# Mamba scan stage of a sandwich block: convolution by stacked taps in four column groups, two copies moved to VectorE, a third dBx buffer

## What is computed

```
xc   = silu(causal_conv(x, w[4 taps]) + b)
dt   = softplus(dt_w @ proj(xc)[:64] + dt_b)        B, C = rest of proj(xc), 16 states each
h[n] = exp(dt * A[n]) * h[n] + (dt * xc) * B[n]     (a scan over time, n = 0..15)
y    = sum over n of h[n] * C[n] + D * xc
```

## Time and profile before

| | us |
|---|---|
| median of 3 runs (4640.19 to 4651.91) | 4651.12 |
| the profiled execution | 4640.61 |
| its span, first to last instruction | 4638.7 |
| input projection and front of the scan stage | 0 to 250.8 |
| the 16 units of the scan | 250.8 to 2059 |

### The profile page before, as it was taken

How to read it: one execution, slowest core, us unless ns; L and a number is a source line. 1 busy time by engine, 2 the same in 40 slices (tenths; PEclk the granted TensorE clock), 3 DMA queues, 4 the chain that set the end, 5 groups by cost and what they waited for, 6 DMA issues and landing times. The chain is left out here.

```text
span 4638.7 us, 68636 instructions
## 1 busy us (share of the span) xinstructions
PE 3669.2 (79%) x20726; PEld 2241.8 (48%) x20726; DVE 2843.6 (61%) x4186; ACT 2755.0 (59%) x4377; POOL 1717.7 (37%) x1132
## 2 busy tenths in 40 slices
PE   8488888888888888866776888888988885499990
PEld 4256666666666666654553222222222223366660
DVE  4268787777777787756675666666666665411105
ACT  3289898988989898964663455555555551011110
POOL 0067777777777777763342000000000002300006
PEclk9799999999989999987886899999999997699995
DMA  6311111111111111114645000000000103311115
GB/s 209 111 44 58 56 56 56 65 56 56 56 56 56 56 60 61 56 74 152 214 154 163 17 24 24 26 24 20 24 26 24 26 17 116 122 61 68 69 41 184
DMA packets 151474, 329.26 MB, mean 71 GB/s; under 512 B 17443, under 2 KB 92310, under 8 KB 136656
## 3 DMA queue, kind: packets, MB, share of 16 engines
q1 hardware_dynamic: 97392, 229.08, 14.6%
q10 hardware_dynamic: 39760, 51.81, 3.3%
q0 software_dynamic: 13968, 43.97, 2.8%
HBM read 216.45 MB, written 110.91 MB: 71 GB/s over the span
## 5 line engine op out<-in xcount | busy, mean ns | idle before, releaser
L671 DVE TENSOR_TENSOR_SCAN scan_hh<-scan_dA,scan_state,scan_bx 128x512 f32<-128x512 f32 x1024 | 1247.1, 1265 | 390.5 <-PE scan_bx L755 350.2
L471 POOL TENSOR_TENSOR scan_hC<-scan_hh,scan_cbc 128x1024 f32<-128x1024 f32 x512 | 1208.2, 2369 | 309.2 <-DVE scan_hh L671 234.2
L1403 DVE TENSOR_REDUCE attend_mx<-attend_s 128x1 f32<-128x512 f32 (+1 forms) x1360 | 781.3, 608 | 343.3 <-PE attend_s L1533 225.1
L755 PE MATMUL scan_bx<-kept_ident,scan_dBxT 128*128 128x128 f32 x4096 | 671.7, 290 | 151.4 <-DVE scan_hh L671 125.3
L755 PEld LDWEIGHTS scan_bx<-kept_ident,scan_dBxT 128*128 128x128 f32 x4096 | 518.0, 150 | 416.0 <-issue 207.9
L538 ACT ACTIVATE scan_dBxT<-scan_dtxT,scan_bt 128x512 f32<-128x512 f32 x1028 | 655.9, 712 | 83.4 <-PE scan_bx L755 83.2
L533 ACT ACTIVATE scan_dA<-scan_dt,scan_an 128x512 f32<-128x512 f32 x1028 | 655.4, 711 | 0.0
L765 PE MATMUL scan_acc<-kept_ident,scan_hC 128*128 128x128 f32 x4128 | 648.2, 284 | 1.3 <-POOL scan_hC L471 1.3
L1497 ACT ACTIVATE attend_full<-attend_s 128x1024 f32<-128x1024 f32 x384 | 392.0, 1025 | 333.4 <-PE attend_s L1560 329.4
L1533 PE MATMUL attend_s<-attend_kt,attend_qt 96*128 96x512 bf16 (+1 forms) x1360 | 483.6, 373 | 130.4 <-DVE attend_mx L1403 72.6
L765 PEld LDWEIGHTS scan_acc<-kept_ident,scan_hC 128*128 128x128 f32 x4128 | 517.3, 149 | 1.6 <-POOL scan_hC L471 1.6
(11 more groups left out here) (218 smaller groups left out, 4597.6 us busy)
## 6 DMA issues: line engine op xcount, KB each, us to landing
scan_cbc<-scratch_crows SPq DMA_DIRECT2D x64, 1024.0 KB, 4.7
scratch_qk<-mix_heads ACTq DMA_DIRECT2D x64, 384.0 KB, 10.0
scan_xw<-scratch_xin SPq DMA_DIRECT2D x18, 1030.0 KB, 7.3
scratch_y<-scan_uu ACTq DMA_DIRECT2D x17, 1024.0 KB, 3.9
attend_qt<-scratch_qk SPq DMA_DIRECT2D x34, 384.0 KB, 3.7
attend_kt<-scratch_qk SPq DMA_DIRECT2D x34, 384.0 KB, 4.4
mix_yf<-scratch_y SPq DMA_DIRECT2D x10, 1024.0 KB, 8.2
mix_yb<-scratch_y SPq DMA_DIRECT2D x10, 1024.0 KB, 11.8
```

The lines of the kernel that those rows point to most:

```text
L471: pool.tensor_tensor(hC[n % 2][:, ms, :], h[:, ms, :], rows.unsqueeze(1).broadcast_to([P, 2, C]), ALU.mult).then_inc(hc_ok, 1)
L671: dve.tensor_tensor_scan(hh[n % 2][:, m, r], dA[n % 2][:, m, r], bx[bank(j)][:, r], state[:, d, n, m:m + 1], ALU.mult, ALU.add).then_inc(h ...
L755: last = pe.transpose(bx[bank(j)][:, t * P:(t + 1) * P], dBxT[n % 2][:, t, m * P:(m + 1) * P], k["ident"][:, :])
L1403: dve.tensor_reduce(mx[:, t, c:c + 1], s1[v % 2][:, 0:w], AX_X, ALU.max).then_inc(s1_read, 1)
```

## The change

1. **Convolution.** The input of a tile is now loaded four times, once for each tap and shifted by it, into 32 partitions each (`xs[tap*32 ...]`), so that the 128 partitions hold 4 taps of 32 channels, and the free dimension has the 4 groups of channels. One product with a 128x32 stationary operand then sums all four taps of 32 channels. Four such products write 32 partitions of `fr` each.
2. **Loads.** A unit's input comes in 4 tiles of 4 DMAs (256 KB each) in place of one DMA of 1030 KB. `xs` has two buffers, one for even and one for odd tiles. SP's order changes: store and load C first, then tiles 0 and 1, then C groups 2 and 3, then tiles 2 and 3, each behind the convolution that frees its buffer.
3. **VectorE** takes the Relu of each dt product (ScalarE keeps the Abs, which now waits for `relu_ok`) and the four copies of turned dt*x.
4. **Third dBxT buffer.** `spread_b` waits for an earlier n.
5. **Front re-ordered.** All four convolutions of a unit now run in the unit two before it. `silu` moves from after n = 3 to after n = 0, the projection from sub-steps 19 to 22 to 7 to 10, the dt products from 29, 31, 33, 35 to 18, 21, 24, 27, GpSimd's add from after n = 9 to after n = 6, and VectorE's three long passes, before after n = 10, 10, 11, now stand after n = 8, 9, 10. On ScalarE exp, 1+e, log and several copies now stand between `spread_b` and `decay` (`middle`).
6. **Chunks** are unrolled in Python on all engines; only the loop over the two batches is left.

```diff
-        xw = [s.sb(f"xw{i}", [P, DT, C + HALO]) for i in range(2)]
-        diag = s.sb("diag", [P, 2, DT, TAPS, P])
+        xs = [s.sb(f"xs{i}", [P, COLS, C]) for i in range(2)]
+        pick = s.sb("pick", [P, STRIP])
+        taps = s.sb("taps", [P, 2, DT, COLS, STRIP])
...
-        dBxT = [s.sb(f"dBxT{i}", [P, JT, DI]) for i in range(2)]
+        dBxT = [s.sb(f"dBxT{i}", [P, JT, DI]) for i in range(3)]
...
-        FR_CONV, FR_PROJ, FR_BT, FR_DT, FR_NEXT, FR_TURN, FR_ALL = 0, 2, 3, 4, 8, 10, 14
+        FR_PROJ, FR_BT, FR_DT, FR_NEXT, FR_TURN, FR_LAST, FR_ALL = 0, 1, 2, 6, 9, 13, 14
+        FR_BEGIN = 18
+        AT_DT, AT_NEXT, AT_TURN, AT_LAST, AT_SKIP = (18, 21, 24, 27), (30, 36, 41), (49, 51, 53, 55), 58, (14, 16, 19, 22)
...
-                with eng.Fori(0, NC) as c:
+                for c in range(NC):
...
+                for tap in range(TAPS):
+                    o = at + tap
+                    sp.dma_start(xs[m % 2][tap * STRIP:(tap + 1) * STRIP, :, :], xinv[b, m, :, :, o:o + C]
+                                 ).then_inc(loaded_x[m % 2], 16)
...
+            for m in range(2):
+                load_x(0, 0, 0, m)
+            for m in range(2, DT):
+                sp.wait_ge(fr_mm, m - 1)
+                load_x(0, 0, 0, m)
+            for m in range(2):
+                sp.wait_ge(fr_mm, m + 3)
+                load_x(0, 0, 1, m)
+            for m in range(2, DT):
+                sp.wait_ge(fr_mm, 14 + m - 1)
+                load_x(0, 0, 1, m)
...
+                        store_c(f, d)
+                        sp.wait_ge(stored_c, f * 16 + 16)
+                        for g in range(2):
+                            load_c(f, d, g)
+                        sp.wait_ge(fr_mm, first)
                         hold(sp, k)
+                        for m in range(2):
+                            load_x(nb, nc_, d, m)
+                        for g in range(2, 4):
+                            load_c(f, d, g)
+                        for m in range(2, DT):
+                            sp.wait_ge(fr_mm, first + FR_NEXT + m - 1)
+                            hold(sp, k)
+                            load_x(nb, nc_, d, m)
...
-                act.wait_ge(fr_mm, group + 1)
-                act.activation(ee[:, m, :], fr[:, :], ACT.Abs, bias=db[:, d, m:m + 1])
-                act.activation(dt[d][:, m, :], fr[:, :], ACT.Relu, bias=db[:, d, m:m + 1]).then_inc(fr_out, 1)
+                act.wait_ge(relu_ok, f * DT + m + 1)
+                act.activation(ee[:, m, :], fr[:, :], ACT.Abs, bias=db[:, d, m:m + 1]).then_inc(fr_out, 1)
...
+                def middle(n):
+                    if n == 2:
+                        for half in range(2):
+                            evacuate(f, half)
+                    if n == 3:
+                        proj_out(g, first + FR_PROJ)
+                    if n == 4:
+                        bt_out(o, first + FR_BT)
+                    if n in (5, 6):
+                        dt_out(o, g, n - 4, first + FR_DT + n - 4)
+                    if n == 7:
+                        front_exp(g, first + FR_DT + 3)
+                    if n == 8:
+                        front_one_plus(g)
+                    if n == 9:
+                        front_log(g)
+                    if n == 11:
+                        conv_out(d, f + 2, 2, first + FR_NEXT + 2)
+                    if n == 15:
+                        conv_out(d, f + 2, 3, first + FR_LAST)
+
+                def tail(n):
+                    if n == 0:
+                        silu(o, g, first - 1)
+                    if n == 3:
+                        store(f)
+                    if n == 4:
+                        dt_out(o, g, 0, first + FR_DT)
+                    if n == 6:
+                        dt_out(o, g, 3, first + FR_DT + 3)
+                    if n in (8, 9):
+                        conv_out(d, f + 2, n - 8, first + FR_NEXT + n - 8)
+
...
-                    act.wait_ge(bx_mm, q * DT + HELD_BX)
+                    act.wait_ge(bx_mm, f * SUB + turned_free(n + 1 if n + 1 < NS else NS))
                     spread_b(dn, at)
+                    middle(n)
                     for m in range(DT):
                         decay(dn, q + 1, at, m)
+                    tail(n)
...
+            def relu(d, f, m, group):
+                if m == 0 and not (isinstance(f, int) and f == 0):
+                    dve.wait_ge(dt_ok, f)
+                dve.wait_ge(fr_mm, group + 1)
+                dve.tensor_scalar(dt[d][:, m, :], fr[:, :], db[:, d, m:m + 1], 0.0, ALU.add, ALU.max
+                                  ).then_inc(relu_ok, 1)
+
+            def turned_out(d, j, group):
+                dve.wait_ge(fr_mm, group + 1)
+                dve.tensor_copy(dtxT[d][:, j, :], fr[:, :]).then_inc(fr_out, 1)
+
...
-            def conv(d, group, nth, m, taps):
-                for j in taps:
-                    if j == 0:
-                        if m == 0:
-                            pe.wait_ge(loaded_x[d], nth * 16 + 16)
-
-                        if not (isinstance(group, int) and group == 0):
-                            pe.wait_ge(fr_out, group)
-                    o = j if d == 0 else HALO - j
-                    last = pe.matmul(fr[:, :], diag[:, d, m, j, :], xw[d][:, m, o:o + C], start=j == 0,
-                                     stop=j == TAPS - 1)
-                    if j == TAPS - 1:
-                        last.then_inc(fr_mm, 1)
+            def conv(d, group, u, m):
+                pe.wait_ge(loaded_x[m % 2], (u * 2 + m // 2 + 1) * 16 * TAPS)
+
+                if not (isinstance(group, int) and group == 0):
+                    pe.wait_ge(fr_out, group)
+                for g in range(COLS):
+                    last = pe.matmul(fr[g * STRIP:(g + 1) * STRIP, :], taps[:, d, m, g, :], xs[m % 2][:, g, :],
+                                     start=True, stop=True, skip_group_check=True)
+                last.then_inc(fr_mm, 1)
```

More of the change, by code:

```diff
@@ L420, in _ @@
                         f = (b * NC + c) * 2 + d
-                        sp.wait_ge(fr_mm, f * FR_ALL + 4)
-                        hold(sp, k)
[L424 to L437, removed]
+                        first = f * FR_ALL + FR_BEGIN
+                        nb, nc_ = (b, c + 1) if c + 1 < NC else (1 - b, 0)
+                        store_c(f, d)
[3 more added lines that the diff above has]
+                        sp.wait_ge(fr_mm, first)
+                        hold(sp, k)
+                        for m in range(2):
[6 more added lines that the diff above has]
+                            load_x(nb, nc_, d, m)
         @block.gpsimd
@@ L454, in _ @@
                 pool.memset(state[:, :, :, :], 0.0).then_inc(zeroed, 1)
-                with pool.Fori(0, NC) as c:
+                for c in range(NC):
                     for d in range(2):
@@ L564, in _ @@
             front_log(0)
-            for j in range(JT):
-                turned_out(0, 0, j, 10 + j)
-            for m in range(2):
+            for m in range(DT):
                 conv_out(1, 1, m, 14 + m)
@@ L581, in unit @@
                     if n + 1 == NS:
-                        act.wait_ge(fr_out, first + FR_ALL)
-                    act.wait_ge(bx_mm, q * DT + HELD_BX)
+                        act.wait_ge(fr_out, first + FR_TURN + JT)
+                    act.wait_ge(bx_mm, f * SUB + turned_free(n + 1 if n + 1 < NS else NS))
                     spread_b(dn, at)
-                    if n == 2:
-                        for half in range(2):
-                            evacuate(f, half)
+                    middle(n)
                     if n + 1 == NS:
@@ L655, in times_x @@
                 dve.tensor_tensor(dtx[:, :, :], dt[d][:, :, :], xc[d][:, :, :], ALU.mult).then_inc(front_ok, 1)
+            def relu(d, f, m, group):
[7 more added lines that the diff above has]
+                dve.tensor_copy(dtxT[d][:, j, :], fr[:, :]).then_inc(fr_out, 1)
+            for m in range(DT):
+                relu(0, 0, m, 6 + m)
             softplus_low(0, 0)
@@ L659, in _ @@
             times_x(0, 0)
+            for j in range(JT):
+                turned_out(0, j, 10 + j)
             def scan(d, f, n, m):
@@ L679, in unit @@
                         scan(d, f, n, m)
+                        at = n * DT + m
+                        if at in AT_DT:
+                            i = AT_DT.index(at)
+                            relu(o, g, i, first + FR_DT + i)
+                        if at in AT_TURN:
+                            i = AT_TURN.index(at)
+                            turned_out(o, i, first + FR_TURN + i)
+                    if n == 8:
+                        softplus_low(o, g)
+                    if n == 9:
+                        softplus(o, g)
                     if n == 10:
[L681 to L683 removed]
                         times_x(o, g)
@@ L738, in _ @@
             for m in range(DT):
-                conv(0, m, 0, m, range(TAPS))
+                conv(0, m, 0, m)
```

(6 more changed lines are left out.)

115 lines of the change are left out of this document (51 added, 64 removed).

## The result

The changed kernel took 4655.88 us (median of 20 runs, 4643.95 to 4669.53) against 4642.63 for the kernel before in the same session (20 runs, 4627.99 to 4652.63). The ratio is 1.003, interval 1.0019 to 1.004. The forecast was 4512, range 4430 to 4600. The profiled execution has a span of 4654.6 us.

A forecast was written before the change was run, and what follows sets the result against it. ScalarE was taken as the bound: 96.2 us work plus 8.3 idle gives a 104.5 us unit; 16 units plus 3.4 make 1675 against 1808, -133. With +4 for the front, 4640.6 becomes 4512, range 4430 to 4600.

The forecast's parts named there:

- the jumps back: Chunk loop: engines start late at each jump back; seven such boundaries, one remains, for which 3.4 us is added.
- the front: Before the first scan: cheaper diagonals against later loads of tiles 2 and 3, net -7 to +15 us, taken as +4.
- TensorE's 9.6 us a unit: Four convolutions a unit: column groups run beside each other, 9.6 us less TensorE work, priced at nothing since TensorE isn't the bound.
- The third dBxT buffer takes away the wait for TensorE: Before `spread_b`: third buffer removes ScalarE's wait, but `decay` waits for the scan instead; alone it earns 0 to 2.92 us.
- the 5.2 us a unit: ScalarE's wait for TensorE before `spread_b` in the kernel before, 83.2 us over 16 units, forecast to go.
- the 0 to 2.92: Range in us for what the third dBxT buffer earns alone, as `decay`'s wait for the scan two states back remains.
- The lateness of tile 2: Load of x for sub-step 41: ready 19.2 to 22.2 us after exp, needed at 20.2; late by 0 to 2, taken 1.0.
- first sign of being wrong: TensorE idle before its third convolution of a unit, with a DMA as releaser, for over 3 us.
- The rival of the late pieces: x loads: four pieces in a row take 14.8 us, not 7.3, so the tile is 9.5 late; 4648 us, chance 9%.
- the surplus of VectorE's busy half: n = 8 to 14: VectorE's extras 14.0 less ScalarE's 5.7 and the 4.7 lead leave ScalarE waiting 3.6 us a unit.
- before Abs (3.2 forecast): dt products: Abs waits for Relu, Relu for the third next scan; ScalarE waits 3.2 us a unit, bounds 0 and 8.8.
- the rival of the single bank: `fr` bank: ScalarE a block behind VectorE makes each of four Abs 2.45 us late, 9.8 a unit; 4669 us, chance 7%.

The follow-up runs named there:

- e8: e4 with only the four Relus of a unit back on ScalarE, VectorE keeping the copies: 4455.2 us, ratio 0.9604.
- e1: Changed kernel with the unit-end spread of B waiting for n = 12 to be turned instead of n = 15: 4586.77 us, ratio 0.988.
- e15: e8 with the wait at the unit's end as strict as in the changed kernel: 4527.07 us, ratio 0.975.
- e7: e4 with dBxT in two buffers as before: 4501.32 us, ratio 0.9692.
- e14: e8 with dBxT in two buffers as in the kernel before: 4462.51 us, ratio 0.9609.
- e2: Changed kernel with ScalarE's copies of the first two convolutions behind the decays of n = 7 and 8, not 8 and 9: 4631.27 us, ratio 0.998.
- e3: Changed kernel with tiles 2 and 3 of x loaded before C's fourth group: 4608.13 us, ratio 0.9938.
- e4: Changed kernel with e1, e2 and e3 together: 4499.43 us, ratio 0.97.
- the three edits: e1, e2 and e3 together on the changed kernel, run as e4: 4499.43 us, ratio 0.97.
- e12: Changed kernel as it is, with only the four Relus of a unit back on ScalarE: 4622.21 us, ratio 0.9953.
- e13: e8 with ScalarE emptying the accumulator earlier, behind n = 1: 4453.26 us, ratio 0.9595.

## Why the prediction was wrong

**What held.** ScalarE is the engine nearest to the unit's length, and the change takes 4 us of its work away: 96.7 measured, 96.2 forecast. The convolution's eight records take 1.06, the jumps back cost 28 us for 20, the front 2.8 for 4. TensorE's 9.6 us a unit are saved too, as e8's 83.2 against 92.8 shows; in the changed kernel, with more of it at the lower clock, it is busy for 86.4.

**The step that failed.** "The third dBxT buffer takes away the wait for TensorE", and with it the 5.2 us a unit, was wrong: the wait rose to 8.7. The buffer was read from what the edit is for, and its slots at the unit's end were not worked out. Two spreads wait there. The one for n = 15 writes the slot of n = 13, two states back as with two buffers: 4.1 of the 8.7 us. The one for the next unit's first state takes its count from `turned_free(16)`, the slot of n = 15, and so waits for all 64 sub-steps, while with two buffers it stopped at n = 14: 4.6 us. This second one is 69 us of the kernel's time (e1), and 72 with the rest mended (e15). With that count mended, the buffer as it stands in this ring is worth nothing (e7 and e14), the lower end of the 0 to 2.92 that the prediction gave it by itself.

**The step that was left out.** The prediction followed the `fr` bank through the dt products, but not through the convolutions: the first one's product stands at sub-step 30, the second's at 36, and between them ScalarE's copy stands behind the decays of its step n = 8. TensorE arrived 6.5 us too early, every unit (e2, 25 us alone).

**A term that was mis-sized.** The lateness of tile 2 was 4.8 us in the unit shown and 3.9 on average, not 1.0 (e3, 48 us alone); this was the prediction's own first sign of being wrong. The supply was right: from the end of exp at 869.8 to TensorE's start at 891.6 are 21.8 us, forecast 19.2 to 22.2. The demand was wrong: TensorE wanted the tile at 886.8, 17.0 after exp, not 20.2. VectorE's long passes took 2.29 and 2.98 in that unit, not 4.4. The price that the prediction took from the Trainium skill, "SBUF — State Buffer", section "Door 1: The DMA port swizzle", and left out of its sum, was 13.6 us for the four pieces of a tile, 6.3 more than for one load. The trace doesn't bear it out: TensorE starts on tile 2 at 891.57, 9.2 us after the first of its pieces was issued at 882.34. One load of 1030 KB landed in 7.3 before; a single piece of 256 KB takes a median of 7.8 (6.3 in e3), so a piece is no faster than the whole, but the pieces overlap. The rival of the late pieces (4648) came nearest to the measured time by chance: the lateness it rests on, 9.5 us, did not come.

**Two agreements that are luck.** The first is the 3.4 us of `decay` behind the scan, forecast at 3.6 as the surplus of VectorE's busy half. It shrinks to 2.0 us a unit in e2 and 1.1 in e3 and is gone in e4, with VectorE's work all in place: it came from TensorE's two stands, not from VectorE's passes. The second is the sum. The changed kernel's 4656 less the three edits is 4499, where 4512 was forecast, and e4 has 7.9 us of idle time a unit for 8.3. But 4.7 of it are before Abs (3.2 forecast) and 3.0 before the spread for n = 15 (nothing forecast), while the 3.6 for VectorE's busy half and the 1.0 for tile 2 are gone. Two terms too small and two too large nearly cancel.

**The moved work.** (It is four Relus and four copies a unit; the "two copies" of the title are the two kinds.) Two costs were put on the eight operations: their work, hidden under ScalarE's, and 3.2 us before Abs. The wait was 4.5. But taking the Relus back gave 34 us here (e12) and 44 with the three edits (e8), though ScalarE then works 2.0 us a unit more. Priced against the sum of work, a Relu on VectorE saves 0.57; in the measured time, that saving included, it costs 44 / 64 = 0.7 for each of the 64 Relus. It goes with the wait before Abs, which falls from 4.7 us a unit to 0.3. Abs stands behind Relu by the program's choice; whether both could read the bank unordered for less was not tried.

**Together.** The convolution's hold and the Relu hand-over are of the kind of the rival of the single bank (4669), but the largest cause, e1, is none of it; no rival had it. What e2 and e3 are worth with only the other missing was not tried. Nor was the clock taken apart from the waits: the mean granted clock of the scan stage was 0.93 before, 0.90 in the changed kernel, 0.94 in e4 and 0.95 in e8, so part of what the edits give back may be TensorE's faster work once it stands less.

The version that beats both kernels is e8 (4455.2, ratio 0.9604), or e13, which is the same within its spread.

## What to carry to other kernels

Where several engines run hand-ordered programs through one bank or one ring of buffers, work out for each waiting instruction its count at the wrap-around, and for each group in which position of which program the releaser stands. A sum of work said that some 130 us were to be had, and e4 has some 140; one wrong index, one copy a state too late and one load behind another took all of it back. Look twice before two readers of one PSUM bank are put on two engines, one behind the other, to save half a microsecond: here the second engine's wait for the first cost more than that, 44 us in 64 banks. And where a total agrees with the forecast, hold its terms against the waits one by one before it is called right.

## What was not expected of the hardware

Two of VectorE's long passes, with both inputs in SBUF, took about half as long in the changed kernel. Lines 644 and 650 of before took 4.37 and 4.40; the same passes are lines 685 and 691 here, with 2.29 and 2.63 on average (lines 702 and 707 are the new Relu and copy):

```profile
L702 DVE TENSOR_SCALAR scan_dt<-scan_fr,scan_db 128x512 f32<-128x512 f32 x64 | 46.4, 726 | 0.0
...
L707 DVE COPY scan_dtxT<-scan_fr 128x512 f32<-128x512 f32 x64 | 42.6, 666 | 0.0
L691 DVE SCALAR_TENSOR_TENSOR scan_dt<-scan_dtx,scan_ee 128x2048 f32<-128x2048 f32 x16 | 42.1, 2630 | 0.0
...
L685 DVE SCALAR_TENSOR_TENSOR scan_ee<-scan_uu,scan_dt 128x2048 f32<-128x2048 f32 x16 | 36.7, 2293 | 18.0 <-ACT scan_uu L556 18.0
```

The time did not vanish. GpSimd, beside the pass of 876.63 to 878.92 on VectorE:

```profile
874.39 2.36 POOL L507 TENSOR_TENSOR scan_hC<-scan_hh,scan_cbc 128x1024 f32<-128x1024 f32 x1
876.69 2.27 POOL L505 COPY scan_state<-scan_hh 128x4 f32<-128x4 f32 x1
878.93 4.70 POOL L507 TENSOR_TENSOR scan_hC<-scan_hh,scan_cbc 128x1024 f32<-128x1024 f32 x2
```

Its copy of four elements a partition, 0.19 us where no such pass is beside it, took 2.27, until VectorE's pass was over. Before, GpSimd had come first:

```profile
885.59 2.37 POOL L471 TENSOR_TENSOR scan_hC<-scan_hh,scan_cbc 128x1024 f32<-128x1024 f32 x1
887.90 2.25 POOL L469 COPY scan_state<-scan_hh 128x4 f32<-128x4 f32 x1
```

VectorE's pass of 885.73 began 0.14 us behind the start of that product and took 4.37, to 890.10; the copy, next on GpSimd, then stood until the pass was over. Whichever came first ran at its own speed and the other stood still. It is the order and not the kernel: in e4 line 685 is back at 4.17 on average, and in the unit looked at a product of GpSimd started at 833.76, the pass at 834.12. The Trainium skill, "SBUF — State Buffer", section "Who interferes with whom", states that a VectorE instruction with two SBUF inputs contends with a GpSimd instruction that reads SBUF, and that the order of issue decides who is blocked; by that rule, the traces agree. VectorE was busy for 89.7 us a unit, not the forecast 94.4, with all eight operations added; the two passes are 3.9 of the 4.7. GpSimd was busy for 88.0 instead of 85.9, and its copies of the state are 1.9 of that.
